# Decoder layer: ternary feed-forward weights made piece by piece through an HBM scratch

## The reference, cut to what matters

```
# A: channel attention (512 x 512 scores over channels), weights Wq, Wk, Wv, Wo
# B: attention of 16 heads (8 groups of 2) over the sequence and over 64 context rows,
#    fp8-rounded inputs, layernorm of every head; output projection wproj
# C: feed-forward, ternary weights
def quant_weight(w):                       # one scale for the whole matrix
    scale = clip(mean(abs(w)), EPS)
    return clip(round(w / scale), -1, 1) * scale
def quant_act(x):                          # one scale for a row
    s = 127 / clip(max(abs(x), axis=-1), EPS)
    return clip(round(x * s), -128, 127) / s
h = quant_act(x) @ quant_weight(w_gate_up).T       # 512 -> 2 x 2048
a, b = split(h)
y = quant_act(silu(a) * b) @ quant_weight(w_down).T  # 2048 -> 512
```

## Time and profile before

| | |
|---|---|
| median of three runs | 1865.3 us |
| the profiled execution's own time | 1863.95 us |
| its span (first to last instruction) | 1861.9 us |
| PE busy | 1761.9 us (95%) |
| DVE busy | 1442.0 us (77%) |
| ACT busy | 1096.4 us (59%) |
| POOL busy | 269.2 us (14%) |
| HBM read, written | 63.47 MB, 4.19 MB |

### The profile page before, as it was taken

The page is one execution under the profiler, slowest core; times in us unless marked ns, Lnnn a source line. Parts: engine busy times, 40 slices in busy tenths (PEclk is TensorE's granted clock), DMA queues, the critical chain, the costliest instruction groups (busy, mean ns, idle before and its releaser), DMA issues.

```text
span 1861.9 us, 31969 instructions
## 1 busy us (share of the span) xinstructions
PE 1761.9 (95%) x10933; PEld 1249.6 (67%) x11048; DVE 1442.0 (77%) x4621; ACT 1096.4 (59%) x2526; POOL 269.2 (14%) x417
## 2 busy tenths in 40 slices
PE   9999999369999999999999999999999999879998
PEld 4444454248777787778877787778877777644554
DVE  1235525578888888888888888888879888879997
ACT  1141422436766667766676666776666676667776
POOL 0000000111211212112111111111111121101111
PEclk9999999689999999999999999999999999989999
DMA  6000000211102001110110100111010102210000
GB/s 226 23 6 17 1 0 2 79 57 37 35 25 59 24 26 46 36 37 13 59 35 25 54 29 25 47 37 36 2 48 1 48 24 90 71 46 13 28 25 29
DMA packets 40495, 70.77 MB, mean 38 GB/s; under 512 B 2960, under 2 KB 21904, under 8 KB 39312
## 3 DMA queue, kind: packets, MB, share of 16 engines
q1 hardware_dynamic: 40336, 68.73, 11.4%
HBM read 63.47 MB, written 4.19 MB: 36 GB/s over the span
## 4 chain that ended last, share of the span: by engine, by line
PE 71%; DVE 15%; issue 9%; ACT 3%; POOL 2%; DMA 0%; POOLq 0%; DVEq 0%; ACTq 0%
PE bank L467 15%; PE bank L521 10%; PE bank L577 8%; PE bank L616 5%; PE bank L541 4%; PE bank L652 3%; PE bank L369 3%; PE bank L454 3%; PE bank L430 3%; PE bank L448 3%; PE bank L419 3%; PE bank L527 3%; PE bank L500 2%; PE bank L398 2%; PE bank L494 1%
## 5 line engine op out<-in xcount | busy, mean ns | idle before, releaser
L890 ACT ACTIVATE pr<-bank,nmx 128x512 f32<-128x512 f32 x256 | 175.0, 692 | 141.8 <-DVE nmx L1235 141.5
L467 PE MATMUL bank<-wqs,XQ 128*128 128x256 f16 x2048 | 248.6, 275 | 4.4 <-DVE x L1159 4.4
L521 PE MATMUL bank<-prT,KV 128*128 128x256 f32 x1024 | 244.6, 382 | 0.1
L577 PE MATMUL bank<-kT,qT 128*128 128x512 f32 x512 | 243.0, 597 | 0.7 <-ACT kT L823 0.7
L467 PEld LDWEIGHTS bank<-wqs,XQ 128*128 128x128 bf16 x2048 | 199.1, 99 | 45.0 <-issue 15.5
L521 PEld LDWEIGHTS bank<-prT,KV 128*128 128x128 f32 x1024 | 191.2, 192 | 52.1 <-issue 22.8
L1380 POOL TENSOR_TENSOR rdev<-gvar,cst 128x7 f32<-128x7 f32 x128 | 193.2, 1510 | 10.0
L878 ACT ACTIVATE yb<-bank,rsT 128x128 bf16<-128x128 f32 x512 | 146.7, 373 | 62.3 <-PE bank L527 62.3
L1378 POOL TENSOR_TENSOR gvar<-mvB,geps 128x7 f32<-128x7 f32 x128 | 29.0, 227 | 1041.5 <-DVE mvB L1119 1034.6
L1235 DVE TENSOR_REDUCE nmx<-bank 128x1 f32<-128x512 f32 x256 | 166.6, 680 | 10.5 <-PE bank L577 7.4
L616 PE MATMUL bank<-identf,pr 128*128 128x128 f32 x1024 | 152.1, 277 | 15.4 <-DVE pr L1139 14.8
(11 more groups left out here) (164 smaller groups left out, 3197.4 us busy)
## 6 DMA issues: line engine op xcount, KB each, us to landing
wst<-in_wcat SPq DMA_DIRECT2D x24, 512.0 KB, 3.9
wpst<-in_wproj SPq DMA_DIRECT2D x8, 1024.0 KB, 5.3
wa<-in_wgu SPq DMA_DIRECT2D x16, 512.0 KB, 3.5
xT<-in_xT SPq DMA_DIRECT2D x4, 1024.0 KB, 7.0
wkx<-in_wkvx SPq DMA_DIRECT2D x8, 512.0 KB, 4.8
wa<-in_wdn SPq DMA_DIRECT2D x8, 512.0 KB, 3.6
wst<-in_wgu SPq DMA_DIRECT2D x4, 1024.0 KB, 5.1
wqs<-in_wgu SPq DMA_DIRECT2D x4, 1024.0 KB, 5.0
```

Source lines behind the costliest of these rows:

```text
L467: ins = mm(dst, XQ[:, b, c, k, j * P:(j + 1) * P], w, start=(k == 0 and m == 0), stop=(k == KT - 1 and m == 1))
L521: mm(OB[:, 0:2 * P], KV[:, n % 2, t, P:2 * P], prT[:, st % 2, t, :, :].rearrange("p h s -> p (h s)"), start=(t == 0), stop=(t == ST - 1))
L577: mm(SB_[h][:], qT[:, h, st * P:(st + 1) * P], kT[:, :], start=True, stop=True).then_inc(s["scores_made"], 1)
L890: act_f(pr[:, h, :], SB_[h][:], ACT.Exp, bias=nmx[:, st, h:h + 1], accum_out=su[:, st, h:h + 1]).then_inc(s["exp_done"], 1)
```

## The change

The turns are cut in half, moved out of the last head group and sent through HBM.

- A piece is now 128 x 1024 (24 instead of 12). `SUMS` puts the sums of absolute values into tiles 0 to 23, so four in each of the pairs 0 to 5. The all-reduce moves from pair 24 to pair 6, `means_ready` from pair 25 to 7.
- `TURN` places a turn in tiles (b, st) = (1, 1), (2, 1), (2, 3), (3, 1), (3, 3) of the head groups 2 to 6, 24 in all.
- In a turn ScalarE scales the piece (with the per-partition `winv`) and then takes the constant off, two ACTIVATEs one behind the other. VectorE only clips, one tile later. The piece lives in `wa`, the buffer of the sums; its rounded form `wt` overlies the first half.
- SP stores the piece to an HBM scratch (`store_tern`) and loads the next raw piece when the store has landed (`load_tern`).
- In pairs 28 to 30 `fetch_tern` loads the finished weights in three DMAs of 2 MB.
- The first tiles of stage C are prepared earlier: `x_stats` in T = 117, 119, 122, 125, `x_norm` in T = 118, 120, 123, `x_prepare` in T = 119, 121, 126, `turn_x` in T = 125 and 126. The buffers of stage C are ordered so that these are free by then.
- TensorE waits for the three fetches ahead of `gate_up` and `down` in place of `tern_made`.

```diff
+SUMS = {i: i for i in range(NABS)}
+TURN = {16 * g + 4 * b + st: i for i, (g, b, st) in enumerate(
+    [(g, b, st) for g in range(2, NG - 1) for b, st in ((1, 1), (2, 1), (2, 3), (3, 1), (3, 3))][:NABS])}
+XSTAT = {4 * NB * NG + o: t for t, o in enumerate((-11, -9, -6, -3))}
...
+            def load_tern(i):
+                if i:
+                    sp.wait_ge(s["tern_stored"], 16 * i)
                 else:
+                    sp.wait_ge(s["abs_made"], NABS)
+                dst = wa[:] if i < NABS1 else wa[:].rearrange("p (k n) -> p k n", k=2)
+                sp.dma_start(dst, piece(gu_cols, dn_cols, i)).then_inc(s["tern_read"], 16)
+            def store_tern(i):
+                sp.wait_ge(s["tern_made"], i + 1)
+                src = wt[:] if i < NABS1 else wt[:].rearrange("p (k n) -> p k n", k=2)
+                sp.dma_start(piece(scr_gu, scr_dn, i), src).then_inc(s["tern_stored"], 16)
+            def fetch_tern(i):
+                if i == 0:
+                    sp.wait_ge(s["tern_stored"], 16 * NABS)
+                sp.wait_ge(s["proj_q_made"], 4 * (TT - 3 + i))
+                sp.wait_ge(s["proj_kv_made"], 3 * (TT - 3 + i))
...
+                if TT - 4 <= n < TT - 1:
+                    fetch_tern(n - (TT - 4))
+                for T in range(4 * n, 4 * n + 4):
+                    if T in SUMS:
+                        if SUMS[T] + 1 < NABS:
+                            load_abs(SUMS[T] + 1)
+                        else:
+                            load_tern(0)
+                    if T in TURN:
+                        store_tern(TURN[T])
+                        if TURN[T] + 1 < NABS:
+                            load_tern(TURN[T] + 1)
...
-                    if n == TT - 1 and st == 3:
-                        turn_x(0, 0)
+                    if n == TT - 1 and st in (1, 2):
+                        if st == 1:
+                            pe.wait_ge(s["xs_sub"], TT)
+                        turn_x(st - 1, st - 1)
...
-            turn_x(1, 1)
-            pe.wait_ge(s["tern_made"], 8)
+            pe.wait_ge(tern_loaded[0], 16)
+            pe.wait_ge(tern_loaded[1], 16)
             gate_up(0, 0, 0, True)
...
+            def tern_scale(i):
+                w = 0 if i < NABS1 else 1
+                if i == 0:
+                    act.wait_ge(s["winv_ready"], 1)
+                act.wait_ge(s["tern_read"], 16 * i + 16)
+                act_f(wa[:], wa[:], ACT.Copy, scale=winv[:, w:w + 1], bias=INT_ROUND).then_inc(s["tern_scaled"], 1)
+            def tern_round(i):
+                act.wait_ge(s["tern_scaled"], i + 1)
+                act_f(wt[:], wa[:], ACT.Copy, bias=-INT_ROUND).then_inc(s["tern_int"], 1)
...
-                        if n < NABS:
-                            sum_abs(n)
+                    if T in SUMS:
+                        sum_abs(SUMS[T])
+                    if T in TURN:
+                        tern_scale(TURN[T])
+                        tern_round(TURN[T])
...
-                    if (n, st) in TURN:
-                        c = TURN[n, st]
-                        if c:
-                            tern_clip(c - 1)
-                        tern_scale(c)
-                    if n == TT - 1 and st:
-                        x_prepare(st - 1, (st - 1) % 2)
-                    if n == TT - 1:
-                        x_stats(st)
+                    if T - 1 in TURN:
+                        tern_clip(TURN[T - 1])
+                    if T in (4 * TT - 9, 4 * TT - 7, 4 * TT - 2):
+                        x_prepare((4 * TT - 9, 4 * TT - 7, 4 * TT - 2).index(T), 1)
+                    if T in XSTAT:
+                        x_stats(XSTAT[T])
```

More of the change, by code:

```diff
@@ L176, in build @@
         y = sb(stC, "y", [P, 2, D])
+        yo = sb(stC, "yo", [P, 2, D])
+        hb = sb(stC, "hb", [P, F], BF16)
+        hT = sb(stC, "hT", [P, FT, P], BF16)
         xi = sb(stC, "xi", [P, D])
@@ L214, in build @@
         s = {n: sem(n) for n in names}
-        chunk_loaded = [sem(f"chunk_loaded{i}") for i in range(2)]
+        tern_loaded = [sem(f"tern_loaded{i}") for i in range(3)]
         out_stored = [sem(f"out_stored{i}") for i in range(2)]
@@ L332, in _ @@
                     copy_vx((n + 1) // 2)
+                if b == 1 and g + 1 < NG:
+                    load_context(g + 1)
+                if TT - 4 <= n < TT - 1:
[10 more added lines that the diff above has]
+                            load_tern(TURN[T] + 1)
                 if b == 0 and g + 1 < NG:
                     load_out(g + 1)
[L335 to L344, removed]
                 if b < 3 and 3 * (g + 1) + b + 2 < 3 * NG:
@@ L1199, in x_prepare, with tern_clip @@
                 scales(t, 0)
-                if par or not (isinstance(t, int) and t == 0):
+                if t:
                     dve.wait_ge(s["xi_made"], t)
                 v.tensor_scalar(xi[:], x1[:, t, :], am2[:, t % 4, 2:3], INT_ROUND, ALU.mult, ALU.add).then_inc(s["xi_added"], 1)
[L1204 to L1211, removed]
+            def tern_clip(i):
+                dve.wait_ge(s["tern_int"], i + 1)
+                v.tensor_scalar(wt[:], wt[:], 1.0, -1.0, ALU.min, ALU.max).then_inc(s["tern_made"], 1)
             def sums_ready():
@@ L1222, in means_ready @@
                 own.sync()
-                own.do(v.reciprocal(winv[:], wsc[:]))
-                own.sync()
+                v.reciprocal(winv[:], wsc[:]).then_inc(s["winv_ready"], 1)
             def pair(g, b, first, last):
@@ L1295, in _ @@
             accumulate(LT - 2, 14)
-            tern_clip(11)
             def h_make(t, par, j):
@@ L1380, in deviations @@
                 g.tensor_tensor(rdev[:], gvar[:], CPOW, ALU.pow).then_inc(s["stats_ready"], 1)
[L1382 to L1403, removed]
             def deviation(slot, var, count, used, done):
@@ L1422, in of_y, with pair @@
                 deviation(1, s["varY_ready"], t + 1, s["yo_ready"], s["rstdY_ready"])
+            def pair(gr, b, first, last):
+                n = 4 * gr + b
+                nxt = not (last and b == 3)
+                for st in range(ST):
+                    T = 4 * n + st
+                    if nxt:
+                        deviations(4 * n + 4 + st)
+                    if T in XSTAT:
+                        of_x(XSTAT[T])
+                    if n == 6 and st == 1:
+                        pool.wait_ge(s["abs_ready"], 1)
+                        g.partition_all_reduce(asum3[:], asum2[:], P, RADD).then_inc(s["absum_ready"], 1)
+            pool.wait_ge(s["yA_made"], ST * NB)
+            g.memset(VB[:], 0.0).then_inc(s["vx_cleared"], 1)
+            for j in range(4):
+                deviations(j)
+            for b in range(NB):
+                pair(0, b, True, False)
+            for gr in range(1, NG - 1):
+                for b in range(NB):
+                    pair(gr, b, False, False)
+            for b in range(NB):
+                pair(NG - 1, b, False, True)
             NT = NB * ST
-            for t in range(4):
-                of_x(t)
             for t in range(NT):
```

67 lines of the change are left out of this document (25 added, 42 removed).

## The result

The changed kernel takes **1848.26 us** (median of 4 runs, 1847.31 to 1850.32); the kernel before, measured beside it, 1864.57 (the three runs of above and one more). The ratio is 0.9913, with a 95% interval of 0.9896 to 0.993. In the profiled executions the span goes from 1861.9 to 1845.5 us, 16.4 less; the profiled execution of the changed kernel is the fastest of its four.

What follows compares the result with a forecast made beforehand. TensorE was taken to set the pace in steady pairs, VectorE and its chain behind pair 31's `px`. -9.0 - 8.6 + 6.0 = -11.6 takes 1863.95 to 1852.4; with the median 1.35 higher, forecast 1853.5 us, range 1849 to 1857.5.

Steps and rivals of the forecast that it cites:

- full cover: Rival: ScalarE's turns in the steady pairs cost 1 us or less, giving 1848; chance 0.16.
- step 2: Pair 31's `px` to the first `gate_up`: less VectorE work gains 8.6 us, bounds 5 and 10.2.
- late round trips: Rival: scratch stores and the loads behind them take 10 us, 12 us on top, about 1863; chance 0.06.
- Step 1: Pairs 28 to 30: turns leave, stages of first feed-forward tiles enter; net gain 9.0 us, bounds 5.6 and 11.3.
- Step 3: Turns in steady pairs delay ScalarE's exponentials: cost 6.0 us, all at tile 3, none at tile 1; bounds 0 and 26.4.
- No cover: Rival: each turn's ScalarE scaling delays `pr` and TensorE waits; price 26.4 us, giving 1874; chance 0.10.
- Step 4: VectorE's clip in tile 2 or 0: about 0.4 us each, cost 0, undiminished 9.6.
- Step 5: Sums of absolute values four to a pair, in tiles 0 to 23: cost 0, upper bound 3 us.
- Step 7: DMAs of the pieces' round trips and the three 2 MB fetches: cost 0; store 2.0 us, load 3.5.
- Step 6: All-reduce in pair 6 instead of 24: its 6.12 us move with it, effect 0, bounds -1 and +1.

Runs made afterwards that it cites:

- Experiment 3: The changed kernel with the first feed-forward tiles of stage C prepared in pair 31, as in the kernel before: 1851.96 us, ratio 0.9933.
- experiment 4: The changed kernel without a turn's scaling pass on ScalarE (weights rounded unscaled; clip, store, load and waits stay): 1843.46 us, ratio 0.989.
- Experiment 11: Experiment 10's kernel with `x_stats` at T = 116, 120, 124, 127 and `x_prepare` at T = 118, 122, 126: 1839.89 us, ratio 0.9869.
- experiment 7: The changed kernel with turns at (0, 0), (1, 1), (2, 1), (3, 1) of groups 2 to 6, the last four in pairs 28 and 29: 1843.72 us.
- experiment 5: The changed kernel with a turn's scaling on VectorE and only the rounding on ScalarE: 1849.54 us, ratio 0.9918.
- experiment 2: The kernel before with the sums four to a pair in tiles 0 to 23 and the all-reduce in pair 6: 1864.23 us against 1863.75.
- the repeat: The changed kernel run again, unaltered: 1848.72 us (5 runs) against 1864.69, ratio 0.9916.
- experiment 10: The changed kernel with the all-reduce behind tile 3 of pair 6 and the turns placed as in experiment 7: 1838.52 us, ratio 0.986.
- experiment 1: The kernel before with only the sums moved, four to a pair in tiles 0 to 23: 1863.97 us against 1863.75, ratio 1.0002.

## Why the prediction was right, and where it was not

The forecast of 1853.5 is 5.2 above the measured 1848.26. That lies just outside the forecast's own range (1849 to 1857.5) and inside the wide one (1847 to 1862). By the table 2.3 of the 5.2 are the end's, 2.2 the all-reduce's and 0.5 the last group's. The direction and the two sources, the end and the last group, were right. The time that came, 1848, is that of the rival "full cover", but its mechanism is not: the turns did cost 5.9 us. That the time agrees with it is chance.

Three sums of the prediction are off, none by much. 1863.95 - 11.6 + 1.35 is 1853.7, not 1853.5. In step 2 the 3.4 of tile 1 counts as 3.2, without which the gain is 8.8. And "late round trips" counts ten turns at tile 3 where the plan has nine.

*Step 1, the last group: right in sum (-9.53 for -9.0), wrong in its parts.* I took 117.30 as the pace without turns. Experiment 3 shows 115.51, 1.8 less. Most of it, 1.25, is the last distance, 38.13 for 39.38. There TensorE has less to do, since the last pair has no projections for a next one. First a batch 2 to 3 at pace (experiment 4), then pair 30 to 31 of experiment 3:

```profile
1425.53:1464.91 39.38, 38.69 (x287) 31.41 (x287) 35.45 (x128) 27.45 (x70) 6.94 (x8) 1.00 0.14 41
1587.46:1625.59 38.13, 35.68 (x249) 27.77 (x248) 33.74 (x121) 22.50 (x56) 7.93 (x12) 1.00 0.01 1
```

The step named this ("may now profit from it is not counted") and put it at nothing. The other two distances are 0.26 shorter each, where the splits of weights are missing; that these make it is not shown. Against that the x work costs 3.5, not 2.2: pair 29 to 30, with T = 117 and 119, loses 1.9 (predicted 1.6, and the wait of 1.70 for `pr` is there), but pair 30 to 31, with T = 121 and 122, loses 1.6 where I had 0.6. What I overlooked is the wait of 1.16 for `accumulate` at 1608.82: VectorE reaches TensorE not by `pr` alone. The trace of the kernel before could have told me, with its wait of 2.04 at 1567.52. Experiment 11 shows the same operand at another tile.

*Step 2, the end: mechanism right, term too small (-10.93 for -8.6).* I counted 10.2 us of VectorE's work and let only 2.8 of the last 4.2 through, since a chain of TensorE's was to be late next. In fact the stretch got shorter by as much as VectorE's 10.96, and TensorE's busy time fell by 4.4, from 24.53 to 20.09, at a clock of 1.00 for 0.85. The upper bound of 10.2 was worked out without a gain in clock and was passed. 20.09 us of full-clock work would take 23.6 at the mean of 0.85, so by this estimate some 3.5 of TensorE's 4.4 us are clock; the other 6.5 of the 10.93 are TensorE's waits, 9.60 before and 3.11 after. Experiment 3 points the same way: with part of VectorE's work still there the clock is 0.89, and 5.2 us less of that work gave 3.8, while the 5.75 that went next gave 7.14. So VectorE's work did not come through one for one; that 10.96 and 10.93 agree is the sum of a part that gave less and one that gave more, where the clock came back. No run takes the work out and keeps the clock, or the reverse.

*Step 3, ScalarE's turns: right (+5.88 for +6.0), and nearly so place by place.* The distances grew by 0.80 from batch 2 to 3 (0.8 predicted) and by 0.42 from batch 3 to 0 (0.5). But in group 6, which has no turn at tile 3 of batch 3, the latter still grew by 0.14. That is the tail of the turn before it: beside experiment 7, TensorE falls behind by 0.95 us there, and `px`, which marks the pair, by only 0.81. So a turn at tile 3 of batch 2 costs some 0.95 and one at tile 3 of batch 3 some 0.28, where I had 0.8 and 0.5; at tiles 1 it is 0. The two passes took 2.2 us from first start to the next start, 1299.69 to 1301.89, as estimated. Experiment 4 shows that it is ScalarE's lateness and not clip, store or load; experiment 7, that it is the place and not the number. "No cover" would have had losses at tile 1; "full cover" none at tile 3. The rule of the Trainium skill ("ScalarE: Activation LUTs", Rules for kernel authors) that mul and add belong on VectorE was put to the test in experiment 5: 1849.54 against the changed kernel's 1848.26, so no gain here. The factor of about 3 stands there for bf16; for these float32 pieces the traces have 0.75 us against 1.20, a factor of 1.6. The timing for an ACTIVATE in the Trainium skill ("ScalarE: Activation LUTs", What ACT_TABLE_LOAD costs) gives, as an estimate, about 1.13 us for L876; the trace has 1.20.

*Step 4, the clip: right.* 0.394 each, nothing lost (experiment 4). *Step 5, the sums:* 0.2 us, for 0. *Step 7, the DMAs: right.* Store 2.0, load 3.8, no wait of ScalarE; "late round trips" is out.

*Step 6, the all-reduce: this was the step that failed.* "The 6.12 move with it" assumed that the step is a fixed price of the same GpSimd work. At pair 24 it was 6.12 and 6.69, at pair 6 it lay between 3.95 and 5.45 in seven profiles. Windows of 20 us around it, and TensorE's wait for `nq` inside, first in the kernel before (pair 24):

```profile
1365.00:1385.00 20.00, 16.40 (x94) 13.35 (x94) 13.88 (x45) 10.60 (x27) 3.43 (x4) 0.83 0.02 3
```

```profile
1369.38 1.09 PE L506 MATMUL bank<-identf,kn 128*128 128x128 f32 x4 [3.38 <-DVE nq L1129]
```

in the changed kernel (pair 6):

```profile
664.00:684.00 20.00, 16.14 (x112) 12.97 (x112) 15.05 (x50) 11.16 (x30) 3.43 (x4) 1.00 0.09 26
```

```profile
668.28 0.63 PE L523 MATMUL bank<-identf,kn 128*128 128x128 f32 x4 [3.03 <-DVE nq L1157]
...
676.86 0.66 PE L635 MATMUL bank<-identf,pr 128*128 128x128 f32 x4 [0.77 <-DVE pr L1167]
```

and in experiment 4, the same place:

```profile
664.00:684.00 20.00, 16.94 (x106) 13.20 (x106) 14.98 (x50) 10.71 (x29) 3.42 (x4) 0.91 0.04 6
```

```profile
668.56 0.63 PE L523 MATMUL bank<-identf,kn 128*128 128x128 f32 x4 [3.06 <-DVE nq L1155]
```

The step is a wait of 3.0 to 3.9 us, and what a lower granted clock behind it adds; in the changed kernel's profile, with the clock at 1.00, it is the 3.03 and a second wait of 0.77, for `pr`. The wait does not decide the clock: 3.03 left it at 1.00, 3.06 came with 0.91. Why pair 24 has 0.83 in both profiles and pair 6 has 0.91 to 1.00 stays open. Moving the all-reduce is worth 0.7 to 2.7 us by these profiles, and no time of a whole kernel shows it (experiment 2). Since the stretches differ by a us or so between executions, part of the 5.2 by which the forecast missed is not the change's at all: in the repeat, with a step of 5.35, the parts add up to 15.0.

## What to carry to other kernels

Put optional work by the idle time in front of the next instruction that another engine waits for, tile by tile: the same turn cost 0 at tile 1 and 0.9 at tile 3 of batch 2, and placing the turns and the all-reduce in this way gave 9.7 us on top of the change's 16.3. An instruction's busy time is no measure of how long it holds its queue: the all-reduce shows 0.41 us and takes about 13. When work is moved into a tile that looks free, list every operand by which that engine feeds TensorE (here `pr` and `accumulate`), and not only the one that was late last.

## What the hardware did that was not expected

In pair 31 one wait of TensorE of 1.91 us came with a granted clock of 0.88 around it (0.50 from 1636 to at least 1639), while two of 0.82 and 1.21 in the same stretch kept it at 1.00 (experiments 11 and 10). At the all-reduce, waits of nearly one length (3.03 and 3.06) stood beside clocks of 1.00 and 0.91, so the length of the last wait alone does not tell what follows. The tail of stage C says the same: behind 1.64 us of waiting the clock stood at 1.00 in experiment 1 and at 0.72 in experiment 2, over 5 us, and the stage came out 1.65 us longer there. A fetch of 2 MB from the scratch took 7.5 us from issue to landing, and none of the three delayed TensorE.
